# Masked attention of the second layer: head groups weighed in two blocks of a batch instead of four

## What is computed

```
q = (layernorm(x) @ wq.T + bq) -> 16 heads of 16     # per batch 112 rows
k, v = (ctx @ wk.T + bk), (ctx @ wv.T + bv)          # per batch 375 rows
scores = clip(q @ k.T * scale, -100, 100)
scores = where(mask == 0, -inf, scores)
x = x + tanh(g) * (softmax(scores) @ v @ wo.T + bo)
```

## Time and profile before

| what | value |
|---|---|
| median of 3 runs | 1407.85 us (1407.03 to 1411.52) |
| span of the profiled execution | 1407.5 us |
| masked attention in it, from the first turn of the maxima on | about 396 to 700 us |
| one body of it, from turn to turn | 18.7 to 18.9 us, the first 19.70, the last 19.19 |
| TensorE busy | 1309.7 us (93%) |
| VectorE busy | 1105.5 us (79%) |

### The profile page before, as it was taken

One profiled execution on the slowest core, in us unless ns is written; L12 is line 12 of the kernel. 1 busy time (PEld: TensorE's weight loads), 2 busy tenths in 40 slices (PEclk: granted clock), 3 DMA queues, 4 the chain that ended last, 5 costly groups with the idle time before them and its releaser, 6 DMA issues. The chain is left out here.

```text
span 1407.5 us, 36465 instructions
## 1 busy us (share of the span) xinstructions
PE 1309.7 (93%) x11864; PEld 977.1 (69%) x11864; DVE 1105.5 (79%) x3711; ACT 693.9 (49%) x1639; POOL 415.0 (29%) x580
## 2 busy tenths in 40 slices
PE   5999999899899999999799889999988998997998
PEld 3777888645467777776545568878867887885766
DVE  7798778678779998888678867767665886668997
ACT  2666677544345555555333356766762323332322
POOL 2332346444433344446134423432420000000000
PEclk8999999999989999999899999999999998999999
DMA  5544455231333333334011233333347351550000
GB/s 170 158 121 117 138 147 147 82 113 49 85 98 99 94 85 93 90 88 128 16 53 50 77 106 106 86 96 102 87 132 205 124 172 45 140 148 25 16 15 23
DMA packets 134073, 138.11 MB, mean 98 GB/s; under 512 B 38601, under 2 KB 121292, under 8 KB 133836
## 3 DMA queue, kind: packets, MB, share of 16 engines
q1 hardware_dynamic: 133948, 136.51, 33.8%
HBM read 100.98 MB, written 35.48 MB: 97 GB/s over the span
## 5 line engine op out<-in xcount | busy, mean ns | idle before, releaser
L1143 DVE TENSOR_REDUCE negm<-ps 112x1 f32<-112x375 f32 x512 | 260.3, 542 | 107.4 <-PE ps L1267 105.6
L1267 PE MATMUL ps<-kst,qst 96*112 96x375 f16 x768 | 232.5, 338 | 13.9 <-DVE negm L1143 8.1
L853 ACT ACTIVATE p<-ps 125x448 f32<-125x448 f32 x336 | 177.3, 543 | 109.3 <-PE ps L1295 72.0
L1282 PE MATMUL ps<-qst,kst 112*125 112x224 f16 (+1 forms) x1152 | 209.9, 264 | 8.2 <-POOL qst L822 4.3
L822 POOL TENSOR_TENSOR qst<-m_row,diag 16x448 f16<-16x448 f16 x128 | 130.2, 1046 | 280.1 <-ACT m_row L932 274.5
L1282 PEld LDWEIGHTS ps<-qst,kst 112*125 112x125 f16 (+1 forms) x1152 | 146.6, 138 | 43.4 <-issue 9.5
L1773 PE MATMUL ps<-fw,xs_e 128*128 128x512 f16 x672 | 162.4, 385 | 0.0
L1127 DVE TENSOR_SCALAR ps<-ps 125x448 f32<-125x448 f32 x192 | 120.1, 629 | 31.1 <-PE ps L1282 31.0
L1139 DVE CUSTOM_DVE_ANT_0 with_mask<-ps,mask_add 112x375 f16<-112x375 f32 x256 | 134.3, 545 | 11.5 <-issue 10.1
L1267 PEld LDWEIGHTS ps<-kst,qst 96*112 96x112 f16 x768 | 97.2, 131 | 46.6 <-DVE negm L1143 20.7
L1190 PE MATMUL ps<-wkv_split,ctxT 128*125 128x256 f16 x864 | 121.6, 278 | 1.1 <-DVE ks L1098 1.1
(11 more groups left out here) (262 smaller groups left out, 2507.2 us busy)
## 6 DMA issues: line engine op xcount, KB each, us to landing
k_split<-ks SPq DMA_DIRECT2D x48, 375.0 KB, 3.5
kst<-k_split SPq DMA_DIRECT2D x96, 187.5 KB, 2.9
fw<-in_w SPq DMA_DIRECT2D x16, 1024.0 KB, 7.2
qst<-q_split SPq DMA_DIRECT2D x96, 112.0 KB, 2.4
kst<-k_split SPq DMA_DIRECT2D x96, 93.8 KB, 2.7
stage<-in_ctxT SPq DMA_DIRECT2D x16, 375.0 KB, 3.9
ctxn<-in_ctx SPq DMA_DIRECT2D x16, 375.0 KB
rows<-x SPq DMA_DIRECT2D x48, 112.9 KB, 2.5
```

Of the source, the lines that this page charges most:

```text
L853: act.activation(p[p_of[hg]][kt], ps[0:KR, BK_ST + n % 2, 0:4 * S], ACT.Exp).then_inc(s_exp, 1)
L1143: dve.tensor_reduce(g.negm[1 - par][:, h:h + 1], scored, AX_X, ALU.max, negate=True).then_inc(s_max, 1)
L1267: mm = pe.matmul(ps[0:S, BK_S + h % 2, 0:SK], g.q_stack[q][0:96, h, :], g.k_stack[q][0:96, h // 2, :], start=True, stop=True)
L1282: mm = pe.matmul(bank[:, 2 * r * S:2 * (r + 1) * S], g.k_stack[par][0:rows, pr, kt * KR:(kt + 1) * KR], g.q_stack[par][0:rows, 2 * pr:2 * ...
```

## The change

In the plan of the masked attention `weigh` becomes 14, 14, 28, 28 (it was 12, 14, 28, 30), and the turn of the maxima goes from slot 30 to slot 28.

```diff
     True: Plan(turned=[0, 2, 4, 6, 8, 10, 12, 14, 16, 18, 20, 22],
                shift=[2, 4, 6, 9, 10, 12, 14, 17, 18, 20, 23, 24],
-               scores=[0, 1, 2, 4, 4, 9, 9, 10, 11, 13, 13, 15, 16, 17, 18, 19], weigh=[12, 14, 28, 30], keys=[1, 4],
+               scores=[0, 1, 2, 4, 4, 9, 9, 10, 11, 13, 13, 15, 16, 17, 18, 19], weigh=[14, 14, 28, 28], keys=[1, 4],
                low=[0, 4], rows=6, q=7, values=[17, 20, 22], turn=11, divide=12, back=16, out=19, update=22,
-               stats=[23, 26, 30], maxima=30, pv=0, split=30, split_low=16, norm=29, xnT=5, q_out=9, k_out=[1, 4],
+               stats=[23, 26, 30], maxima=28, pv=0, split=30, split_low=16, norm=29, xnT=5, q_out=9, k_out=[1, 4],
                v_out=[17, 20, 25], oT=16, m_out=31),
```

## The result

The changed kernel takes 1418.13 us (median of 4 runs, 1417.25 to 1419.11) where before, measured beside it, took 1407.44; the ratio is 1.0065, with a 95% interval of 1.0046 to 1.0084. A second time, 6 runs against 17: 1417.81 against 1410.38 us, ratio 1.0067 (1.0048 to 1.0086). So it is slower, by 7 to 11 us. The forecast was 1413.9 with a range to 1417: the direction is right, the size too small by about a third. The ratio on the median shown before, 1407.85 us, gives 1417.0, the very end of the range; the median itself, 1418.13, lies 1.1 us above it.

What follows compares the result with a forecast made beforehand. VectorE was taken to lead mid-body and TensorE from shift 7. A loss of 0.47 less 0.03 us in most bodies summed to +6.0 us on the 1407.85 median: 1413.9 us, range 1409 to 1417.

Steps and rivals of the forecast that it cites:

- What bounds the kernel: Masked attention body: VectorE leads in slots 12 to 17, TensorE from shift 7 to the body's end.
- The joins, 0.11 us: Two weigh blocks standing together on TensorE take 1.31 us instead of 1.42, saving 0.11 us a join.
- Weigh 0 behind turned score 7, 0.47 us late at shift 7: Mid-body: shift 6 waits for clip 6, so shift 7 comes 0.47 us late per body, bounds 0.35 to 0.60.
- It adds nothing: VectorE gets score 11 0.26 us late, delaying maximum 11 and clip 8; less than TensorE's delay, so no added cost.
- The turn and the second join, 0.03 us: End of body: turn of the maxima ahead of weigh 2, weigh 2 and 3 joined; gains 0.03 us, bounds 0 to 0.11.
- The sum: Over all bodies: 0.44 us in twelve, 0.5 for bodies 2 and 3, 0.2 for body 0; +6.0 us, bounds 3.4 to 8.4.
- counted as like body 11: Bodies 1 and 4 to 14 were each taken to lose 0.47 - 0.03 = 0.44 us.
- the 0.2 us taken: Body 0: VectorE leads up to the last shift, so TensorE's delay is mostly swallowed; 0.2 us lost.
- The clock: Part of the 8% rival that more is lost: clock falling to 0.91 where TensorE leads, 0.6 us a body more.

Runs made afterwards that it cites:

- e1_middle: Against before, only weigh 0 moved, from slot 12 to 14 (turn of the maxima stays in 30): 1419.71 us, ratio 1.0071, 13 inner bodies 248.34 us.
- e8_w0_13: Against before, only weigh 0 moved, from slot 12 to 13, in front of shift 6: ratio 1.0017, 13 inner bodies 246.54 us.
- e4_fill: Against the changed kernel, values 0 of the next batch moved from slot 17 to 13: ratio to before 1.0047, 13 inner bodies 247.44 us.
- e7_split: Against the changed kernel, weigh 1 moved from slot 14 to 15, values 0 left in 17: ratio to before 1.0094, 13 inner bodies 252.03 us.
- e2_end: Against before, only the end moved (weigh 3 and turn of the maxima from slot 30 to 28): ratio 0.9983, run again 1.0009; inner bodies 244.25 us.
- e3_turn_last: Against before, weigh 3 moved from slot 30 to 28, turn of the maxima left in 30: 1414.39 us, ratio 1.0032.
- e4 to e7: Against the changed kernel: values 0 in slot 13; weigh 0, 1 in 13, 13; in 14, 15 with values 0 in 13; in 14, 15. Ratios to before 1.0047, 1.0043, 1.0069, 1.0094.

## Why the prediction was right in direction and short in size

- **What bounds the kernel.** Right in the main: VectorE leads to clip 7, TensorE from shift 7 on; e1_middle and e8_w0_13 bear it out. But TensorE's lead is a small one: relieved of 0.66 us in e4_fill, it waits for VectorE at score 13 and shift 8.
- **The joins, 0.11 us.** Right: the pair takes 1.29 us from its first load to the next instruction's where two alone take 1.42, so 0.13. The rule of the Trainium skill that was weighed (TensorEngine Tiling (Array Packing), Key Properties: a change of mode drains TensorE) agrees with the pair and with e7_split, where splitting it costs 0.28 us; no gap shows in front of a block behind a turned score. It never shows as time, because the place takes more.
- **Weigh 0 behind turned score 7, 0.47 us late at shift 7.** Right in kind, too large in what stays. Shift 6 is not 0.06 us early: its load comes 1.55 us behind shift 5 as before, and 0.35 us of the wait in front of it stand at score 10, for maximum 8, which the prediction did not have. From shift 5 to shift 7 are 3.61 us before and 4.12 after, matmul to matmul, 0.51 us late; load to load, as the prediction counted, it is 3.60 and 3.96, only 0.36 and near its lower bound of 0.35. Of the matmuls' 0.51 us some 0.14 are given back before the last shift, which the prediction did not foresee: 0.05 directly behind shift 7 (0.24 us to the next matmul before, 0.19 after) and 0.09 between shift 8 and the projection out (0.63 against 0.54). The last shift's load stands 8.93 us behind shift 5 instead of 8.55: 0.38 us.
- **"It adds nothing", of VectorE's late maximum 11.** True of the changed kernel, but only because the other delay is larger: it is 0.31 us late, not 0.26. e4_fill takes 0.66 us of work off TensorE behind shift 7, and 0.30 us a body stay. The prediction named one limit where there are two of nearly the same size; its reader would have thought filling the gap a cure, as e4_fill's own expectation did.
- **The turn and the second join, 0.03 us.** Right: 0.02 us at shift 0, 0.00 us in e2_end's bodies, and e3_turn_last shows both reasons.
- **The sum.** For 13 inner bodies the working gives 11 x 0.44 + 0.5 = 5.3 us; measured 4.2 and 4.1. Bodies 4 and 11 to 13 grew by 0.37 us each, body 1 by 0.57; but bodies 5 to 10, counted as like body 11, took 18.80 to 18.94 us before and grew by 0.16 to 0.45 in the first trace, 0.19 to 0.28 in the second. Body 0: 19.70 and 19.65 us before, 19.69 and 19.85 after, no more than the 0.2 us taken.
- **The clock.** Mis-sized, and this is why the whole came out larger: the forecast had none of it in the sum and put it, at 8%, as a fall in the stretch that TensorE leads. The clock stayed at 1.00 in all inner bodies; it fell longer behind them, in body 14 or just behind it. The rests differ by 5.5 to 5.9 us: 0.6 us is the earlier mark, some 0.4 us body 14's own order (an estimate from the inner bodies), and 6 to 13 us more at half the clock are 3 to 6 us. So the sum of 6.0 us owes some of its nearness to luck: it has the 13 bodies 1.1 us too high and the clock at nothing, and the two errors work against each other.

## What to carry to other kernels

In a pipeline of two engines with two banks between them, ask of a block not only how long it is but what stands behind it that the other engine, or the bank's next round, needs: one block per round was free here where it did not stand behind a wait (0.2 us in e8_w0_13, where it did), and two in one round, between two neighbouring shifts, cost 0.3 to 0.65 us a body in each of the five orders tried (changed, e4 to e7). When a wait is found to cost, check whether a second one of nearly the same length stands behind it before filling the first. And compare the two ends of a long loop apart from its inside: the inside agreed to 0.2 us between runs, while the ends, where the clock changes, moved by several us.

## What the runs showed of the hardware

- A block of fp32 matmuls with 32 output columns has a gap of 0.17 us behind it wherever something else follows, and one of 0.17 to 0.20 us in front of it behind a score or a shift (e7_split, e8_w0_13), but none behind a turned score. So its price depends on its neighbours: 0.60 us from block to block, 0.71 us to anything else, and some 0.13 us more behind a score (0.29 us from score 11 to the block, where a score costs 0.16).
- Equal programs differ by 9 us (0.6%) in their runs, from 1405.2 to 1414.7 us over 90 runs of before, and the time goes with the mean granted clock, about 0.57 us for each 0.001 of it (a fitted line; the correlation is 0.70). Inside, at a clock of 1.00, the 13 bodies of its two traces agree within 0.1 us: 244.30 and 244.24.
